# The last product of a fused attention and gated layer, as seven block products

## The reference, cut to what matters

```
def _binary_diff_weight(w, base):
    d = w - base
    coeff = jnp.mean(jnp.abs(d))
    return base + coeff * jnp.sign(d)
gate = einsum('bsh,ih->bsi', hidden_states, W1)
up = einsum('bsh,ih->bsi', hidden_states, W3)
h = jax.nn.silu(gate) * up
return einsum('bsi,hi->bsh', h, W2)
```

## Time and profile before

| | us |
|---|---|
| median of 3 runs | 1353.12 (1345.4 to 1356.75) |
| the profiled execution's own time | 1348.54 |
| its span, first to last instruction | 1346.7 |
| TensorE busy in it | 1225.3 (91%) |
| VectorE, ScalarE, POOL busy | 918.6, 685.5, 362.9 |
| mean granted TensorE clock | 0.957 of full |

### The profile page before, as it was taken

One profiled execution on the slowest core, in us unless ns is written; L12 is line 12 of the kernel. 1 busy time (PEld: TensorE's weight loads), 2 busy tenths in 40 slices (PEclk: granted clock), 3 DMA queues, 4 the chain that ended last, 5 costly groups with the idle time before them and its releaser, 6 DMA issues.

```text
span 1346.7 us, 16946 instructions
## 1 busy us (share of the span) xinstructions
PE 1225.3 (91%) x6292; PEld 959.7 (71%) x6292; DVE 918.6 (68%) x1229; ACT 685.5 (51%) x1037; POOL 362.9 (27%) x243
## 2 busy tenths in 40 slices
PE   4888787788898599999899999999999999979998
PEld 4755454455666487778787888888888888858887
DVE  6778676767777967766467777777775555545553
ACT  4767566464444547667466644444443443324431
POOL 2213132321422213333333332333213222212230
PEclk9999888788999699999999999999999999989999
DMA  9266666663111147877887743344438565566552
GB/s 354 82 235 226 241 235 251 253 247 114 74 63 63 47 147 219 234 229 243 255 235 231 211 152 131 123 153 156 156 119 315 193 201 187 189 197 199 196 188 78
DMA packets 77445, 250.00 MB, mean 186 GB/s; under 512 B 9250, under 2 KB 9524, under 8 KB 76852
## 3 DMA queue, kind: packets, MB, share of 16 engines
q1 hardware_dynamic: 73332, 234.25, 49.0%
q0 software_dynamic: 4032, 14.68, 6.0%
HBM read 225.82 MB, written 23.07 MB: 185 GB/s over the span
## 4 chain that ended last, share of the span: by engine, by line
PE 67%; DVE 13%; DMA 8%; ACT 6%; issue 4%; POOL 1%; SPq 0%; DVEq 0%; ACTq 0%
PE pair L1322 20%; PE pair L1364 11%; PE quad L1364 11%; PE quad L1322 8%; DMA late<-in_w 4%; DMA raw_base<-in_mean_w 2%; DVE negwide L1900 2%; PE quad L1266 2%; PE pair L1303 2%; PE pair L1419 2%; PE quad L1303 1%; PE quad L1256 1%; PE quad L1419 1%; PE pair L1209 1%; PE pair L1194 1%
## 5 line engine op out<-in xcount | busy, mean ns | idle before, releaser
L2238 POOL TENSOR_TENSOR raw_w<-raw_w,raw_base 128x1024 f32<-128x1024 f32 x56 | 141.0, 2519 | 277.5 <-DMA raw_base<-in_mean_w 277.4
L2294 POOL TENSOR_TENSOR v_w<-v_w,v_base 128x512 f32<-128x512 f32 x56 | 82.1, 1466 | 252.2 <-DMA v_base<-in_mean_w 252.2
L2193 DVE TENSOR_TENSOR hop_lo<-hf,hop_hi 128x1024 fp32r<-128x1024 f32 x56 | 68.9, 1233 | 74.4 <-ACT hop_hi L1816 74.4
L1988 DVE SCALAR_TENSOR_TENSOR raw_w<-quad,coeff,raw_base 128x1024 f32<-128x1024 f32 x52 | 66.5, 1279 | 58.0 <-ACT quad L1622 58.0
L1992 DVE TENSOR_TENSOR ring_lo<-raw_base,ring_hi 128x1024 fp32r<-128x1024 f32 x56 | 69.4, 1241 | 48.9 <-ACT ring_hi L1762 44.3
L1800 ACT ACTIVATE v_w<-v_w 128x512 f32<-128x512 f32 x56 | 35.4, 632 | 130.7 <-POOL v_w L2294 130.7
L1322 PE MATMUL pair<-t_b_hi,ring_hi 128*128 128x512 f32 x224 | 90.4, 404 | 9.1 <-ACT snap L1781 9.1
L1322 PE MATMUL pair<-xnT_hi,ring_hi 128*128 128x512 f32 x224 | 88.2, 394 | 10.3 <-DVE t_b_lo L2024 9.8
L1364 PE MATMUL quad<-vop_hi,hop_hi 128*128 128x512 f32 x224 | 88.0, 393 | 5.4 <-DVE outs L2204 5.4
L1816 ACT ACTIVATE hop_hi<-hf 128x1024 fp32r<-128x1024 f32 x56 | 59.1, 1058 | 64.7 <-PE pair L1364 64.5
L1364 PE MATMUL pair<-vop_hi,hop_hi 128*128 128x512 f32 x224 | 87.8, 392 | 1.6 <-DVE outs L2204 1.6
(11 more groups left out here) (322 smaller groups left out, 3147.4 us busy)
## 6 DMA issues: line engine op xcount, KB each, us to landing
raw_w<-in_w SPq DMA_DIRECT2D x56, 512.0 KB, 4.5
raw_base<-in_mean_w SPq DMA_DIRECT2D x56, 512.0 KB, 5.9
hf<-h_rows SPq DMA_DIRECT2D x56, 512.0 KB, 3.3
ctxw<-in_w SPq DMA_DIRECT2D x28, 512.0 KB, 3.9
ctxw<-in_mean_w SPq DMA_DIRECT2D x28, 512.0 KB, 5.2
late<-in_mean_w SPq DMA_DIRECT2D x28, 512.0 KB, 5.0
late<-in_w POOLq DMA_DIRECT2D x28, 512.0 KB, 8.6
h_rows<-work SPq DMA_DIRECT2D x28, 512.0 KB, 6.3
```

Source lines behind the costliest of these rows:

```text
L1988: dve.scalar_tensor_tensor(w[:, :], sign, coeff[:, k:k + 1], base[:, :], ALU.mult, ALU.add).then_inc(f_w, 1)
L2193: dve.tensor_tensor(lo[:, :], hfs[n % HFS][:, :], hi[:, :].bitcast(F32), ALU.subtract).then_inc(hh_lo, 1)
L2238: pool.tensor_tensor(w[:, :], w[:, :], base[:, :], ALU.subtract).then_inc(f_diff, 1)
L2294: pool.tensor_tensor(w[:, :], w[:, :], base[:, :], ALU.subtract).then_inc(v_diff, 1)
```

## The change

The second product is computed with seven block products too. h is cut in four blocks: a11 and a21 are the even groups j for the first and the second half of the tokens, a12 and a22 the odd groups. W2 is cut into b11, b12 (even groups, first and second half of the features) and b21, b22 (odd groups). `SECOND` lists the seven passes: which block of h or sum of blocks (s1 to s4), which place in memory holds the block of W2, and which of two sets of four PSUM banks takes the result. A pass has 14 steps (pairs of groups), and a step four token tiles of three matmuls: 98 steps in all. From pass 5 on the passes add to banks that hold earlier results, which are read in between; `CLEARS` says whose eviction a pass waits for, tile by tile.

- In the first product VectorE makes s1 to s4 from each pair of `held` (u1 to u4, 128x512 each, 56 in all). Seven blocks of 256 KB a pair go to the DRAM tensor h_blocks in five DMAs (sta to ste), in place of two of 512 KB.
- After the Abs of a row of w2 (which now writes into the two spare PSUM banks) ScalarE takes the row's sign as 16-bit numbers (wsgn), and SP stores them, 256 KB a row (gst). The second product reads these signs; it no longer reads w2, and POOL's differences and ScalarE's signs in it are gone.
- The plan issues a row of w2 no sooner than 18 us (`PACE`) after the one before, and loads of the base, the signs and x no sooner than given leads. Its landing times are longer.
- In the second product a load of h brings two steps (512 KB, rows of 2 KB), in three slots. A load of weights brings two steps (512 KB of base in rows of 2 KB and 256 KB of signs in rows of 1 KB) into the block's own place; the 28 such loads fall in the first four passes, VectorE makes the weights in place (bstt), and in passes 4 to 7 it makes sums of them in place (tsum, 28). ScalarE makes both high parts of a step in one instruction (hi, 128x1024), VectorE both low parts (lo, 128x1024), in a ring of three.
- Results: r1, o11, r0, r2, o22, x22, o12 and o21 are VectorE's additions at the ends of passes (128x512, four each), r3 is a copy on ScalarE. They have buffers of their own or are made in place. The rows of x are loaded in two parts of four.

The core of the diff:

```diff
 NAMES = ("w1", "w3", "w2")
 NEED = [(which, j) for j in range(JT) for which in ("w3", "w1")]
-SLOT, FFN_HOP, AHEAD_BY = 2.72, 0.15, 0.5
+SLOT, FFN_HOP, AHEAD_BY, PACE, DELAY = 2.72, 0.15, 0.5, 18.0, 2.5
+LEAD_X, LEAD_B, LEAD_MORE = -5.0, 16.0, 0.6
 PRODUCTS = ("p1", "p2", "p3", "p4", "p5", "p6", "p7")
-LATES, HFS, VS, RINGS, OUTS = 2, 3, 4, 3, 4
+LATES, RINGS, ASLOTS, SIGNS = 2, 3, 3, 4
+PAIRS = JT // PAIR
+TWOS = PAIRS // 2
+BLOCKS = ("s1", "s2", "s4", "s3", "a11", "a12", "a22")
+SECOND = (("a11", "b11", 0), ("a12", "b21", 1), ("s4", "b22", 1), ("s3", "b12", 1), ("s2", "b11", 0), ("s1", "b22", 0), ("a22", "b21", 1))
+GRID = 66
+PLACE = {"b11": 34, "b21": 6, "b22": 48, "b12": 20}
+STAGE = 62
+H_SUMS = {"u1": 1, "u3": 2, "u2": 3, "u4": 4}
+CLEARS = {2: "o11", 3: "r0", 4: "r1", 5: "r2", 6: "o22"}
+STEPS, QTILES = len(SECOND) * PAIRS, TILES // 2
+OUTPUTS = ("o11", "o12", "x22", "o21")
+EVICTIONS = ("r1", "o11", "r0", "r2", "o22", "x22", "o12", "o21")
...
-        add(("store", j), "SP", 0.6, ("h1", j), ("h0", j), previous("store", j), landing=3.0)
-        add(("wload", j), "SP", 0.6, ("wabs", j - LATES), previous("wload", j), landing=3.0)
+        p = j // 2
+        if odd:
...
+            add(("u4", p), "DVE", 0.7, ("u2", p), ("h0", j), ("sta", p), previous("u4", p))
+            add(("stb", p), "SP", 0.6, ("u3", p), previous("stb", p), landing=3.4)
+            add(("stc", p), "SP", 0.6, ("h1", j), ("h0", j), previous("stc", p), landing=4.2)
+            add(("std", p), "SP", 0.6, ("u2", p), previous("std", p), landing=4.2)
+            add(("ste", p), "SP", 0.6, ("u4", p), previous("ste", p), landing=3.4)
+        else:
+            add(("sta", p), "SP", 0.6, ("h0", j), previous("sta", p), landing=3.4)
+        add(("wload", j), "SP", 0.6, ("gst", j - LATES), previous("wload", j), landing=4.2)
         add(("wneg", j), "ACT", 1.05, ("wload", j), previous("wneg", j))
-        add(("wadd", j), "POOL", 0.9, ("wneg", j), previous("wadd", j), landing=6.0)
-        add(("wabs", j), "ACT", 1.25, ("wadd", j), previous("wabs", j))
+        add(("wadd", j), "POOL", 0.9, ("wneg", j), previous("wadd", j), landing=9.0)
+        add(("wabs", j), "ACT", 1.25, ("wadd", j), ("t4lo", 1), previous("wabs", j))
+        add(("wsgn", j), "ACT", 1.05, ("wabs", j), previous("wsgn", j))
...
     add(("csum", 0), "DVE", 0.2, ("wabs", JT - 1))
     add(("coef", 0), "DVE", 0.2, ("cmm", 0))
-    for s in range(2 * JT):
-        freed = (("sum", 4 * JT - 5), ("elo", JT - 2)) if s < 2 else (("flo", JT - 2), ("glo", JT - 2))
-        add(("hload", s), "SP", 0.6, previous("hload", s), *(freed if s < HFS else (("hlo", s - HFS),)), ("store", s % JT),
-            ("store", JT - 5), landing=2.6)
-        freed = ((("flo", JT - 2), ("glo", JT - 2)), (("sum", 4 * JT - 1), ("elo", JT - 1)), (("sum", 4 * JT - 1), ("elo", JT - 1)),
-                 (("flo", JT - 1), ("glo", JT - 1)))
-        add(("vload", s), "SP", 1.0, previous("vload", s), *(freed[s] if s < VS else (("vlo", s - VS),)), landing=2.6)
-        add(("vdiff", s), "POOL", 1.2, ("vload", s), previous("vdiff", s))
-        add(("vsign", s), "ACT", 0.6, ("vdiff", s), previous("vsign", s))
-        add(("vstt", s), "DVE", 0.72, ("vsign", s), ("coef", 0), previous("vstt", s))
-        last = (("h0", JT - 1) if s < JT else ("ev", TILES - 1)) if s % JT == RINGS else None
-        gone = ("st", s - RINGS) if s >= RINGS else ("p7", JT - 1) if s == 2 else ("p2", JT - 1)
-        add(("vhi", s), "ACT", 0.6, ("vstt", s), gone if s >= RINGS else ("p2", JT - 1), last, previous("vhi", s))
-        add(("vlo", s), "DVE", 0.72, ("vhi", s), previous("vlo", s))
-        add(("hhi", s), "ACT", 1.05, ("hload", s), gone, last, previous("hhi", s))
-        add(("hlo", s), "DVE", 1.3, ("hhi", s), previous("hlo", s))
+    stored_by = {"a11": "sta", "s3": "stb", "a12": "stc", "a22": "stc", "s1": "std", "s2": "std", "s4": "ste"}
+    freed = ([("p7", JT - 1), ("gst", JT - 1)], [(x, JT - 1) for x in ("flo", "glo", "elo", "dlo")] + [("sum", 4 * JT - 1)], [("p4", JT - 1)],
+             [("stb", PAIRS - 1), ("stc", PAIRS - 1), ("ste", PAIRS - 1)])
+    for u in range(STEPS // 2):
+        q, i = divmod(u, TWOS)
+        clear = [("lo", 2 * (u - ASLOTS) + 1)] if u >= ASLOTS else [("p2", JT - 1), ("dlo", JT - 2), ("elo", JT - 2), ("sum", 4 * JT - 5)]
+        add(("aload", u), "SP", 0.6, previous("aload", u), (stored_by[SECOND[q][0]], 2 * i + 1), *clear, landing=4.2)
+    for v in range(4 * TWOS):
+        q, i = divmod(v, TWOS)
+        add(("bload", v), "SP", 1.1, previous("bload", v), ("bstt", v - SIGNS), ("p3", JT - 1) if v == TWOS - 1 else None, ("gst", 4 * i + (3 if q in (1, 2) else 2)), *freed[q],
+            landing=5.1)
+        add(("bstt", v), "DVE", 1.28, ("bload", v), ("coef", 0), previous("bstt", v))
+    for u in range(3 * TWOS, STEPS // 2):
+        sources = [("bstt", u - TWOS), ("bstt", u)] if u < 4 * TWOS else [("tsum", u - TWOS)]
+        add(("tsum", u), "DVE", 1.22, previous("tsum", u), *sources)
+
+    def last(q, t):
+        return ("mm", (PAIRS * (q + 1) - 1) * QTILES + t)
+
+    for s in range(STEPS):
+        u = s // 2
+        add(("hi", s), "ACT", 1.05, ("aload", u), ("bstt" if u < 3 * TWOS else "tsum", u),
+            ("mm", (s - RINGS + 1) * QTILES - 1) if s >= RINGS else ("p2", JT - 1), previous("hi", s))
+        add(("lo", s), "DVE", 1.25, ("hi", s), previous("lo", s))
     for t in range(TILES):
-        add(("xload", t), "SP", 0.6, ("p7", JT - 1), previous("xload", t), landing=2.0)
-    for e in range(2 * TILES):
-        add(("ev", e), "DVE", 0.7, ("st", JT - 1 if e < TILES else 2 * JT - 1), ("out", e - OUTS), ("xload", TILES - 1),
-            previous("ev", e))
-        add(("out", e), "SP", 0.6, ("ev", e), previous("out", e), landing=2.0)
+        add(("xload", t), "SP", 0.6, ("p3", JT - 1) if t < QTILES else ("r0", QTILES - 1), previous("xload", t), landing=4.2)
+    for t in range(QTILES):
+        add(("r1", t), "DVE", 0.7, last(0, t), ("xload", t), previous("r1", t))
...
                     product("t4", j, 1.82, *((("t4lo", j - 1),) if j else ()))
                 if q == JT - PAIR and j == JT - 1 and names[0] == "p6":
                     product("cmm", 0, 0.1, ("csum", 0), ("stt", 2 * JT - 1))
-    for s in range(2 * JT):
-        product("st", s, 2 * SLOT, ("vlo", s), ("hlo", s), *((("h1", JT - 1),) if s == 0 else (("ev", 0),) if s == JT else ()))
+    for s in range(STEPS):
+        q, p = divmod(s, PAIRS)
+        for t in range(QTILES):
+            bank_free = [("h1", JT - 1)] if s == 0 and t > 1 else [(CLEARS[q], t)] if q in CLEARS and p == 0 else []
+            product("mm", s * QTILES + t, SLOT / QTILES, ("lo", s), *bank_free)
 
     deps = {key: [x for x in task[3] if x in tasks] for key, task in tasks.items()}
...
+    release = {("wload", j): j * PACE for j in range(JT)}
+    release |= {("xload", t): first + (LEAD_X + 4 * t if t < QTILES else 120.0 + 4 * t) for t in range(TILES)}
+    release |= {("bload", v): first + 2 * SLOT * v - LEAD_B - max(0, v - 2 * TWOS) * LEAD_MORE for v in range(4 * TWOS)}
     order_of = {}
 
     def latest(key):
...
+                q, p = divmod(s, PAIRS)
+                into, found = second_bank[SECOND[q][2]], splits[s % RINGS]
+                pe.wait_ge(a_lo, JT + s + 1)
+                for t in range(QTILES):
+                    if s == 0 and t == 0:
+                        pe.wait_ge(c_ok, 2)
+                        pe.wait_ge(f_w, 2 * JT)
+                    elif s == 0 and t > 1:
+                        pe.wait_ge(h1, JT - 3 + t)
+                    elif s == PAIRS and t < 2:
+                        pe.wait_ge(c21, JT - 1 + t)
+                    elif s == PAIRS:
+                        pe.wait_ge(h0, JT - 3 + t)
+                    elif p == 0 and q in CLEARS:
+                        evicted(pe, CLEARS[q], t)
+                    for n, (a, b) in enumerate(((0, 1), (0, 3), (2, 1))):
+                        a = pe.matmul(into[t], found[:, a, t * P:(t + 1) * P], found[:, b, :], start=p == 0 and n == 0 and q < 4,
+                                      stop=p == PAIRS - 1 and n == 2, skip_group_check=q >= 4)
+                    if p == PAIRS - 1:
                         a.then_inc(o_last, 1)
-                    elif t == TILES - 1:
+                    elif t == QTILES - 1:
                         a.then_inc(o_mm, 1)
...
-                    act.activation(lates[n % LATES][:, :], lates[n % LATES][:, :], ACT.Abs,
+                    act.wait_ge(t4_lo, TILES + 2)
+                    act.wait_ge(f_w, signed)
+                    if n:
+                        act.wait_ge(me_abs, SOON + n)
+                    act.activation(spare.rearrange("p a b -> p (a b)"), lates[n % LATES][:, :], ACT.Abs,
                                    accum_out=absum[:, 2, n:n + 1]).then_inc(me_abs, 1)
...
+                elif task == "wsgn":
```

(43 more changed lines are left out.)

335 lines of the change are left out of this document (213 added, 122 removed).

## The result

| | before | after |
|---|---|---|
| median of 4 runs, us | 1349.26 (1343.56 to 1356.75) | 1293.76 (1287.73 to 1297.21) |
| the profiled execution's own time, us | 1348.54 | 1297.21 |
| its span, us | 1346.7 | 1295.4 |

What follows compares the result with a forecast made beforehand. TensorE was taken to bound the kernel from 478 us on. From the profiled execution, 1348.5 - 38.1 - 10.4 + 5 + 4 - 6 = 1303, plus 2 for the runs' median: 1305 us, range 1289 to 1328, own case 1294 to 1316.

Steps and rivals of the forecast that it cites:

- Matmuls, -38.1: Second product: 168 fewer matmuls at an unchanged 0.2267 us each, -38.1 us.
- The old change of halves, -10.4: Second product: time lost where halves change, to late VectorE evictions and a wait for a store, goes; -10.4 us.
- Four changes of pass, +5: Second product: evictions before passes 3, 4, 6 and 7 cost 1.2 us each, +5; bounds 0 and +14.
- Feeding, +4: Second product, passes 1 to 4: supplying operands, with DMA the tightest resource, costs +4 us; bounds 0 and +16.
- First product, -6: First product: paced w2 rows and longer planned landing recover half of 13 us of snapshot waits, -6; bounds -12, +14.
- (1): Rival: first product gains nothing or loses, as a DMA share of 0.77 holds throughout; 1311 to 1325 us, chance 0.15.
- (2): Rival: feeding decides in passes 1 to 4 if 1 KB packets cost more than 2 KB; 1320 to 1340, chance 0.10.
- (3): Rival: a pair's three loads don't overlap, taking 8.9 us in place of 5.44; +97, 1400 us, chance 0.02.
- (4): Rival: each of four changes of pass waits 10 us as the old change of halves did; 1340 us, chance 0.02.
- (5): Rival: nearly everything hidden and the first product clean; 1289 us, chance 0.10.
- The signs: Listed evidence: second product starts within 1015 to 1025, lasts 270 to 282 us, waits at most 2 us per pass change.

Runs made afterwards that it cites:

- b_outs8: The kernel before with eight output buffers in place of four, nothing else; 1342.02 us, ratio 0.9926.
- b_both: The kernel before with the change's pacing of w2 rows, its longer planned landing times and eight output buffers; 1331.42 us, ratio 0.9848.
- a_slots2: The changed kernel with two buffers for the loads of h in place of three; 1294.20 us, ratio 0.9583.
- b_paced: The kernel before with only the change's pacing of w2 rows and its longer planned landing times; 1339.73 us, ratio 0.9916.
- a_oldland: The changed kernel, pacing kept, with the three planned landing times set back to 4.0, 3.0 and 6.0 us; 1318.15 us, ratio 0.9776.
- a_load7: The changed kernel with the raw loads' planned landing at 7.0 us in place of 6.0; 1291.32 us, ratio 0.9568.
- a_ring2: The changed kernel with two places for split operands in place of three; 1300.72 us, ratio 0.9635.

## Why the prediction was right, and where it was off

**Matmuls, -38.1: right.** 1176 matmuls, 267.47 us for 1176 x 0.2267 = 266.6, the same price as before.

**The old change of halves, -10.4: right, with both causes.** b_outs8 shows the stores as 7.35 of it, and b_both, with the stores gone, still loses some 2.5. What the second product of after still loses is 267.47 - 266.6 = 0.9 us: one wait of 0.47 before pass 7 with its hidden 0.16, and the length of the last matmul.

**Four changes of pass, +5: mis-sized; they cost under 1 together.** I charged 1.2 us each, as if a subtraction of 1.24 us always stood ahead of the first eviction. VectorE's timeline of after, at the change to pass 3:

```profile
1098.99 1.37 DVE L2363 TENSOR_TENSOR grid<-quad,grid 128x512 f32<-128x512 f32 x2 [1.07 <-PE quad L1475]
1100.35 1.37 DVE L2363 TENSOR_TENSOR grid<-pair,grid 128x512 f32<-128x512 f32 x2
1101.64 2.35 DVE L2340 TENSOR_TENSOR split<-grid,split 128x1024 fp32r<-128x1024 f32 x2
```

VectorE waits for TensorE there (1.07 us) with nothing in front; the two subtractions were put behind the evictions, where the ring gives them time. The order is made with the tile's end in it, which the term ignored. Before pass 7, where ScalarE's copy comes between, the slack was worked out as 0.4, and this is the only change that waits:

```profile
1253.71 1.63 PE L1475 MATMUL quad<-split 128*128 128x512 f32 x6 [0.47 <-DVE hid L2347]
```

**Feeding, +4: mis-sized; nothing.** The DMA share of passes 1 to 4 was forecast as 0.83 to 0.94 and is 0.92, 0.69, 0.83 and 0.54: one pass inside, with leftovers from the first product in it, the third at the lower edge, two below. Together that is some 113 us of the 152, where 141 to 158 had been added up. Passes 5 and 6 have 0.28 and 0.29 (0.3 was said). VectorE's fourth pass is 87% busy (91 said), lo takes 1.224 us (1.24 said). I summed packets at prices taken from one kernel's average and then charged unevenness that the buffers absorb: a_slots2 takes one away and loses 1.1, none of it in its first pass, at a share of 0.99.

**First product, -6: right in sign, 2 us short, with part of the cause.** It gained 8.25, of a loss of 13.4 that b_paced proves (13 was said); b_outs8, at 546.10 with this stage untouched, says that 3 us of either number can be the execution's own. ScalarE's waits before the Abs went as said. But the term named the Abs alone, the pacing and the 9.0 us of the accumulating DMA. In before ScalarE stood as long for the plain load of a row's base, before the negation (20.4 us in 10 waits, 6.9 the longest, against 19.0 at the Abs), and the plan's landing of that load went from 3.0 to 4.2. The runs put more on the landing times than on the pacing (20.7 against 4.0 when each is taken back), and the waits that a_oldland brings back are for rows of w2 and, more of them, for raw loads, whose landing the change also raised, from 4.0 to 6.0. How much each of the three landings is worth stays open. The sums on VectorE took 16.2 + 16.0 + 18.8 + 9.7 = 60.7 us, the upper bound of 38 to 62, and cost nothing once the plan holds them. The DMA share is 0.69 in the stage, not 0.77: from b_paced to after it rises by 0.07 of 536 us, 37 us of engine share, where 74 had been added up for the stores.

**The rivals.** (1) fell, but by its own "against" alone: the share of 0.69 holds to the end, as it feared, and the waits come back when the plan's landings are the old ones. a_oldland's first product is 12.4 us longer than before's at a share of 0.69, and its time, 1318.15, is inside this rival's 1311 to 1325; a_load7's is at the floor at a share of 0.71. A milder form of it is real in after, the 5.2 us over the floor. (2) fell: no pass is longer than 38.1. (3) fell: in the first pass loads run side by side, as the DMA view of after for 1024 to 1062 us shows:

```profile
q1 hardware_dynamic: 7402, 12.89, 93.2%
...
grid<-in_mean_w SPq DMA_DIRECT2D x7, 512.0 KB, 5.7
grid<-h_blocks SPq DMA_DIRECT2D x6, 512.0 KB, 5.4
signs<-w_signs SPq DMA_DIRECT2D x7, 256.0 KB, 6.6
```

The three loads of a pair take 5.7, 5.4 and 6.6 us from issue to landing, 17.7 together, and a pair of steps lasts 5.44. The Trainium skill ("DMA: Bandwidth & Descriptors", Bandwidth) asks for DMAs of 1 MiB or more for three quarters of the peak; here 256 and 512 KB each gave 335 GB/s, 77% of its 436, with several under way at a time. (4) fell, no change waits over 0.5. (5), all hidden and 1289, is the nearest of the five; a_load7 is this case, 1291.32.

**The signs.** Most came as listed: the second product starts at 1024.60, and no change waits over 0.5 us. It lasts 267.5 us, under the 270 to 282 of the list, by the two terms that were not paid.

**The total.** The second product was forecast 8.5 us too long (47.97 gained, 39.5 said) and the first 2.2; the untouched part took 5.0 more in the profiled execution, which hides half of this there. The median isn't touched by that and is 11.2 under the forecast. The two large terms measured as forecast; what was wrong, 9 us charged of which under 1 was paid and 2 too little in the first product, lies on one side, and the time is inside the range because the range reached down to rival (5).

## What to carry to other kernels

Where the order on the engines is worked out ahead, its landing times and durations can count for as much as work does: compare each with the median landing in the profile, in the stretch where it is crowded, and set it about there (6.0 against medians of 6.2 and 5.1 was enough in b_paced, 7.0 against 7.3 and 5.8 in a_load7; 6.0 against 7.2 and 5.6 was not, in after). The same additions cost 21.7 us here outside the plan and 2.0 in it. Count what the bounding engine must do and take its floor first; then charge a hand-over only where its slack, worked out with what really stands in front of it in the order, is negative. Buffers between a jumpy supply and a steady consumer swallow waits much longer than a step, so a high DMA share alone is no term.

## What had not been expected

A wait of TensorE can cost twice its length. The table of stretches of after, before the wait of 1.98 us, behind it, and once over it:

```profile
931.00:933.00 2.00, 2.00 (x10) 1.50 (x8) 0.00 (x0) 0.00 (x0) 1.83 (x1) 1.00 1.03 420
935.20:938.90 3.70, 3.67 (x9) 2.94 (x10) 3.70 (x3) 2.75 (x5) 3.23 (x2) 0.55 0.06 23
939.00:941.00 2.00, 2.00 (x10) 1.66 (x9) 2.00 (x4) 0.82 (x3) 0.00 (x0) 1.00 0.00 0
```

The granted clock is 0.55, near the 1.2 GHz level, for 3.7 us, and nine matmuls run in place of sixteen. After the waits of about 0.5 us at the changes of pass in a_ring2 the clock stays at 1.00. The length of the wait alone does not decide it: behind the 3.49 us wait of before the clock is 1.00 (669.6 to 672 us) and only the first matmul is a little long, 0.50 us, so that this wait cost 3.8. Why one wait brings the lower level and a longer one does not, no run separates.

A sum on VectorE that starts behind POOL's difference isn't slowed in proportion; its time looks like standing still until POOL is through. POOL's timeline and VectorE's, of after:

```profile
536.78 2.39 POOL L2396 TENSOR_TENSOR raw_w<-raw_w,raw_base 128x1024 f32<-128x1024 f32 x1 [1.56 <-DMA raw_base<-in_mean_w]
```

```profile
536.17 0.68 DVE L2305 TENSOR_TENSOR s_rows<-work 128x512 f32<-128x512 f32 x1
536.96 2.76 DVE L2309 TENSOR_TENSOR work<-work 128x512 f32<-128x512 f32 x1
540.24 0.68 DVE L2313 TENSOR_TENSOR s_rows<-s_rows,work 128x512 f32<-128x512 f32 x1
```

The sum begins 0.18 us after the difference and ends 0.55 us after it: 2.76 us where its like takes 0.68. The same holds for all eleven of the 56 sums that begin while a difference runs: each ends 0.55 us after it, whether that leaves 2.90 us or 1.08, while sums that began just before a difference, like the one at 536.17, took 0.68 or 0.69. So a mean of 1.1 us, as the prediction used, can be a mixture of 0.7 and up to 2.9. The Trainium skill ("SBUF — State Buffer", SBUF: two separate sides) has this as an exclusive lock between GpSimd and a VectorE instruction with two inputs in SBUF, held for the whole instruction by whichever starts first; the rows agree.

It stays open what a packet of 1 KB costs by itself: no run separates it.
